# Index columns for the gathers of a graph kernel: one copy of all columns behind a step's first gather, in place of one copy behind each gather

## The chip, the cores and the metric

The kernel runs on one core of a Trainium2 chip, in one launch. The metric is the device time of the whole launch in microseconds. A run of the kernel before is 18072.75 us (median of three runs).

## The reference

The model works on a graph of 12,500 nodes and 412,500 edges that are sorted by their destination `dst`; the source `src` of an edge is a random node. Two graph networks run one after the other, each with a residual and a layer norm over the 16 features of a node. Cut to what matters here:

```python
# first network: two graph convolutions of 16 features
xw = x @ W.T
msg = xw[r] * norm[:, None]                      # r = src: a gather of one row per edge
out = jax.ops.segment_sum(msg, c, num_segments=num_nodes)

# second network: encoder, two rounds over the edges, decoder
for s in range(S):                               # S = 2
    ce = jnp.concatenate([e, n[senders], n[receivers]], axis=-1)
    e = e + _ln(_mlp(ce, ...), ...)              # n[senders]: again one row per edge
    agg = jax.ops.segment_sum(e, receivers, num_segments=num_nodes)
    cn = jnp.concatenate([n, agg], axis=-1)
    n = n + _ln(_mlp(cn, ...), ...)
```

Four passes over the edges fetch one table row for the source of every edge: two convolutions (rows of 16 floats) and two rounds (rows of 64 floats).

## The kernel before

The edges are cut into tiles of 128, one edge per partition, and eight tiles make a step (`G = 8`). A pass over the edges is one call of `edge_loop`, with 403 steps (`NIST`). There are four passes, and their tiles carry the names `g1` and `g2` (the convolutions) and `s0` and `s1` (the two rounds); the tiles of g1 and g2 both appear as `g_...` and those of s0 and s1 both as `s_...` in the profile, since numbers are left out of the names. Between the passes lie short phases over the nodes.

Each engine has its own program, a function `step(j, i, b)` that `drive` runs for every step: 19 steps are written out, then a loop on the device runs eight steps per turn, and the last steps are written out again. The engines work on different steps at one time (a lag such as `L_GA = 2` or `3` says how many steps later an engine handles a step), and meet only through semaphores. So in every pass each engine has a fixed order of work and waits for the others.

GpSimd (POOL in the profile) has one duty in a pass: to fetch the rows. For each tile it issues one indirect DMA (`L818`) which reads 128 rows of the table by the 128 node numbers in one column of an index tile `ix[k]`, and writes them to `gt[k]`. There are eight index tiles and eight row tiles, used in turn. The indices of all edges lie in `srcT` on chip; the column of a tile is at an address that depends on the step number. GpSimd therefore copies the columns to `ix`, whose addresses are fixed: behind the gather of tile `s` it copies column `s` of the next step (`L821`). The last copy of a step raises the semaphore `g_ix`.

Before its first gather a step waits (`done`, `landed`) for three things: that the rows in `gt[k]` from eight steps earlier have been used (`v_msg` in g1 and g2, `p_pre` in s0 and s1), that the indices of this step are there (`g_ix`), and that the gathers of seven steps ago have landed (`s_g`). `settle` is one semaphore instruction behind them.

In g1, s0 and s1 a step has eight gathers (`GA = 8`). In g2 it has five, since `xp = 3` tiles of a step take their rows by matmuls with a one-hot matrix from a table that is held on chip: VectorE (DVE) makes the one-hot `g_Oh` (L890), TensorE (PE) multiplies (L1008), DVE picks the rows (`g_sel`, L851, then L857).

Who uses the gathered rows: in g1 and g2 DVE multiplies them with the edge weights into `g_R` (L900); in s0 and s1 PE transposes them (L1033). PE's step in g1 begins with the matmuls of L1022, which need what DVE wrote for an earlier step (L920). Behind the last step of a pass GpSimd issues plain runs of gathers with no copies between them: L829 (`ahead`), and in the node phases L1154 and L1162 (`n_agg`); in the first phases of the kernel L521 (`NA`) is such a run too. `L823` is the copy that fills the first index tile of a pass in one operation.

Of the kernel before, what the change touches and what calls it, by code (L numbers as in the profile page):

```python
# [14 lines left out]
G = 8  # L15
# [45 lines left out]
def build(nc, a, out):  # L61
    ctx = ExitStack()
    with ctx:
        def sbuf(c, name, shape, dt=F32):
            return c.enter_context(nc.sbuf_tensor(name, shape, dt))
# [3 lines left out]
        def mark(name):  # L69
            return Mark(ctx.enter_context(nc.semaphore(name)))  # L70
# [36 lines left out]
        srcT = sbuf(ctx, "srcT", [128, NT + 8 * G], I32)  # L107
# [40 lines left out]
        def lasts_ahead(F):  # L148

            E = {80: 16, 64: 20, 16: 24}[F]  # L150
            return E, ahead[:, 0:E * F].rearrange("p (q f) -> p q f", f=F)
# [490 lines left out]
        def drive(eng, step, tail):  # L642

            for j in range(19):
                step(j, j // 8, j % 8)
            with eng.Fori(2, (NIST - 3) // 8) as i:
                for b in range(3, 11):
                    step(i * 8 + b, i, b)
            for j in range(NIST, NIST + tail):
                step(j, j // 8, j % 8)  # L650
# [5 lines left out]
        def stage(j, off):  # L656

            return not isinstance(j, int) or 0 <= j - off < NIST

        def done(eng, sem, j, off):  # L660

            v = j - (off - 1)
            if not isinstance(v, int) or v > 0:
                eng.wait_ge(sem.sem, v + sem.base)

        def landed(eng, sems, n, i, b, off):

            d = len(sems)
            gen = i * (8 // d) + (b - off) // d
            if not isinstance(gen, int) or gen >= 0:  # L670
                m = sems[(b - off) % d]
                eng.wait_ge(m.sem, (gen + 1) * (16 * n) + m.base)
# [7 lines left out]
        def settle(eng, sem):  # L680

            eng.sem_inc(sem, 1)
# [17 lines left out]
        g_ix, s_blank = mark("e_gix"), mark("e_blank")  # L700
# [3 lines left out]
        def edge_loop(tag, FG, table, seg_d, mlp=None, attr=False, expand=False, zsrc=None, zw=None, zout=None, ew2=None, counted=None, held=None, xp=0):  # L704


            L_GA = 2 if expand else 3
            L_LN, L_SEG = (6, 8) if mlp else (5, 6)
            L_ST = L_SUM = L_SEG + 1
            GA = G - xp  # L710
# [5 lines left out]
            with ExitStack() as c:  # L716
                def many(name, shape, dt=F32, n=2):
                    return [sbuf(c, f"{tag}_{name}{b}", shape, dt) for b in range(n)]
# [6 lines left out]
                ix = many("ix", [128, G], I32, n=8)  # L725
# [80 lines left out]
                def pool(eng):  # L806
                    def step(j, i, b):
                        if stage(j, L_GA):
                            k = (b - L_GA) % 8
                            if expand:  # L810
                                done(eng, p_pre, j, L_GA + 8)
                            else:
                                done(eng, v_msg, j, L_GA + 8)
                            done(eng, g_ix, j, L_GA)
                            landed(eng, s_g, GA, i, b, L_GA + 7)
                            settle(eng, s_m[1])
                            for s in range(GA):
                                eng.indirect_dma_start(out=gt[k][:, s, :], out_offset=None, in_=table[:, :],  # L818
                                                       in_offset=bass.IndirectOffsetOnAxis(ap=ix[k][:, s:s + 1], axis=0),
                                                       ).then_inc(s_g[k].sem, 16)  # L820
                                last = eng.tensor_copy(ix[(k + 1) % 8][:, s:s + 1], srcT[:, bass.ds((j - L_GA + 1) * G + s, 1)])  # L821
                            last.then_inc(g_ix.sem, 1)
                    eng.tensor_copy(ix[0][:, 0:GA], srcT[:, 0:GA]).then_inc(g_ix.sem, 1)  # L823
                    drive(eng, step, L_GA)
                    E, early = lasts_ahead(FS)
                    for k in range(2):
                        eng.wait_ge(*s_so[k](16 * (E * 128 // G // 2)))
                    for q in range(E):
                        eng.indirect_dma_start(  # L829
                            out=early[:, q, :], out_offset=None, in_=seg_d.rearrange("w t f -> (w t) f"),  # L830
                            in_offset=bass.IndirectOffsetOnAxis(ap=lidx[:, q:q + 1], axis=0)).then_inc(s_last[q // 4].sem, 16)
# [853 lines left out]
```

## Time and profile before

| | |
|---|---|
| runs of the kernel | 18072.75 us median of 3 (18071.34 to 18078.55) |
| the profiled execution's own time | 18121.37 us |
| its span, first to last instruction | 18119.2 us |
| GpSimd busy in it | 14425.3 us (80%) |
| TensorE busy | 13301.6 us (73%), mean granted clock 0.702 |
| VectorE busy | 9511.5 us (52%) |
| ScalarE busy | 3049.3 us (17%) |

Times in the profile are microseconds from the start of the span. A group of instructions is shown with its number, its busy time, the mean of one in nanoseconds, and then the time for which the engine stood idle just before them with what ended that idle time ("issue" is time in which the engine waited for nothing that the profile shows). Busy time counts the engine's own instructions; register, branch and semaphore instructions on the engine's sequencer (POOLq is that of GpSimd) are not in it. The chain that ended last is of little use in this kernel, since most of it lies in the last node phase; a pass is read from the waits inside it.

### The profile page before, as it was taken

What the parts mean: (1) busy time and instruction counts of PE and PEld (TensorE: products, weight loads), DVE (VectorE), ACT (ScalarE), POOL (GpSimd) and SP (SyncE); (2) the same over time, 40 slices, a digit from 0 to 9 for tenths busy, and PEclk for the clock granted to TensorE, in tenths of its full rate; (3) what the DMA queues carried; (4) which work ended last, traced back from release to release, by engine and by line L of the source; (5) the groups of instructions that cost most, each with busy time, mean ns of one, the idle gap of its engine ahead of it and who ended that gap; (6) DMA issues with size and microseconds to landing.
All of it is one profiled execution on the core that took longest, in us unless ns stands there. A gap on an engine that the chain in (4) does not pass through costs nothing. (4 is left out here: it accounts for less than half of the span.)

```text
span 18119.2 us, 353439 instructions
## 1 busy us (share of the span) xinstructions
PE 13301.6 (73%) x95144; PEld 10759.4 (59%) x95144; DVE 9511.5 (52%) x28331; ACT 3049.3 (17%) x5120; POOL 14425.3 (80%) x23987
## 2 busy tenths in 40 slices
PE   3777777777689999976777777767667667667775
PEld 2555555555479999974555555555545555555554
DVE  5444444444378888875445454445554444444444
ACT  1222222222200000001111111111111111111111
POOL 6888888888778888876888888888778888888886
PEclk5555555555589999996777777777776776777776
DMA  3222222222211111113555555555444444444442
GB/s 107 60 61 59 61 60 60 61 59 61 61 37 28 27 27 28 27 24 107 147 148 150 147 149 149 146 148 150 119 117 126 125 124 126 124 125 126 125 125 70
DMA packets 1973701, 1714.60 MB, mean 95 GB/s; under 512 B 1266475, under 2 KB 1436319, under 8 KB 1972431
## 3 DMA queue, kind: packets, MB, share of 16 engines
q10 hardware_dynamic: 939256, 958.97, 16.3%
q0 software_dynamic: 394560, 282.16, 9.7%
q1 hardware_dynamic: 639488, 469.70, 9.2%
q14 instruction: 333, 2.73, 0.0%
q8 instruction: 64, 1.05, 0.0%
HBM read 1096.56 MB, written 615.90 MB: 95 GB/s over the span
## 5 line engine op out<-in xcount | busy, mean ns | idle before, releaser
L818 POOL DMA_INDIRECT s_gt<-ta_d,s_ix x6448 | 6329.1, 982 | 1621.3 <-issue 967.9
L818 POOL DMA_INDIRECT g_gt<-xs_d,g_ix x3224 | 3158.7, 980 | 807.0 <-issue 483.6
L687 DVE TENSOR_TENSOR s_P<-psw,dlT 128x1024 f32<-128x1024 f32 x806 | 987.2, 1225 | 4106.8 <-PE psw L1055 4062.8
L1033 PE MATMUL pair<-ident,s_gt 128*128 128x128 f32 x3224 | 781.5, 389 | 2760.8 <-DMA s_gt<-ta_d,s_ix 2759.7
L1008 PE MATMUL pair<-g_part,g_Oh 128*128 128x224 bf16 x25389 | 2542.2, 261 | 238.9 <-DVE g_sel L851 211.7
L1008 PEld LDWEIGHTS pair<-g_part,g_Oh 128*128 128x128 bf16 x25389 | 2431.8, 99 | 279.4 <-issue 203.8
L1055 PEld LDWEIGHTS psw<-s_R,s_P 128*128 128x128 f32 x12896 | 2118.2, 247 | 734.3 <-issue 734.3
L818 POOL DMA_INDIRECT g_gt<-ys_d,g_ix x2015 | 1990.1, 988 | 583.6 <-POOL g_ix L821 325.6
L1033 PEld LDWEIGHTS pair<-ident,s_gt 128*128 128x128 f32 x3224 | 506.2, 194 | 3016.2 <-issue 1873.4
L1055 PE MATMUL psw<-s_R,s_P 128*128 128x64 f32 x12896 | 1998.8, 323 | 2.2 <-DVE s_R L920 1.4
L1055 PEld LDWEIGHTS psw<-g_R,g_P 128*128 128x128 f32 x6448 | 1405.3, 330 | 612.9 <-issue 612.9
L1022 PE MATMUL pair<-e_w,g_hT 128*128 128x128 f32 x3224 | 827.5, 438 | 1078.4 <-DVE g_R L920 1078.4
L900 DVE TENSOR_TENSOR g_R<-g_gt,ew 128x128 f32<-128x128 f32 x806 | 238.5, 296 | 2575.5 <-DMA g_gt<-xs_d,g_ix 2260.2
L1042 PE MATMUL pair<-s_z,zw 128*128 128x512 f32 x1612 | 1523.8, 1044 | 0.0
L1055 PE MATMUL psw<-g_R,g_P 128*128 128x80 f32 x6448 | 1491.8, 426 | 11.3 <-DVE g_R L920 11.3
L1022 PEld LDWEIGHTS pair<-e_w,g_hT 128*128 128x128 f32 x3224 | 717.6, 327 | 1234.6 <-issue 957.0
L821 POOL COPY s_ix<-srcT 128x1 int32 (+1 forms) x6448 | 1294.6, 201 | 41.1
L1039 PE MATMUL pair<-s_Pt,s_Bw 128*64 128x128 bf16 x19344 | 1124.2, 300 | 11.6 <-DVE s_Pt L882 11.6
L965 ACT ACTIVATE g_sg<-psw 128x640 f32<-128x640 f32 (+1 forms) x806 | 395.8, 491 | 4109.4 <-PE psw L1055 4090.3
L1039 PEld LDWEIGHTS pair<-s_Pt,s_Bw 128*64 128x64 bf16 x19344 | 938.1, 161 | 245.3 <-issue 194.1
L821 POOL COPY g_ix<-srcT 128x1 int32 (+1 forms) x5239 | 1052.7, 201 | 33.7
L960 ACT ACTIVATE s_hT<-pair 128x512 f32<-128x512 f32 x806 | 481.7, 598 | 3417.1 <-PE pair L1042 3404.8
(333 smaller groups left out, 18150.3 us busy)
## 6 DMA issues: line engine op xcount, KB each, us to landing
s_dl<-dl_d SPq DMA_DIRECT2D x404, 512.0 KB
seg_d<-s_sg ACTq DMA_DIRECT2D x806, 256.0 KB
s_Bw<-tb_d ACTq DMA_DIRECT2D x3224, 48.0 KB
s_Bw<-tb_d SPq DMA_DIRECT2D x3224, 48.0 KB
seg_d<-g_sg ACTq DMA_DIRECT2D x403, 320.0 KB
z_d<-g_rT ACTq DMA_DIRECT2D x403, 256.0 KB
s_z<-z_d ACTq DMA_DIRECT2D x403, 256.0 KB, 2.8
s_gt<-ta_d,s_ix POOLq DMA_INDIRECT x6448
```

The source lines that it names most:

```text
L687: return eng.tensor_tensor(P[:, :, :], bc(columns.rearrange("p (o e) -> p o e", o=1), [128, G, 128]), bc(dlT[:, bass.ds(j * G, G)].rearran ...
L818: eng.indirect_dma_start(out=gt[k][:, s, :], out_offset=None, in_=table[:, :], in_offset=bass.IndirectOffsetOnAxis(ap=ix[k][:, s:s + 1], a ...
L821: last = eng.tensor_copy(ix[(k + 1) % 8][:, s:s + 1], srcT[:, bass.ds((j - L_GA + 1) * G + s, 1)])
L900: last = eng.tensor_tensor(R[k][:, :, FM:FS], gt[k8][:, :, :], bc(ew2[:, bass.ds((j - L_LN) * G, G)].rearrange("p (s o) -> p s o", o=1), [ ...
L960: eng.activation(hT[k][:, :], ps[k][:, :], ACT.Silu).then_inc(a_h.sem, 1)
L965: eng.activation(sg[k][:, :].rearrange("p (t f) -> p t f", t=G), psw[:, 0:G * SP_].rearrange("p (t f) -> p t f", t=G)[:, :, 0:FS], ACT.Cop ...
L1008: last = eng.matmul(near_out(k, t), Oh[k][:, g, 128 * t:128 * t + 128], part[n][:, g, :, :].rearrange("p f l -> p (f l)"), start=g == 0 an ...
L1022: eng.matmul(ps[2 + k][:, 128 * q:128 * q + 128], hT[k][:, 128 * q:128 * q + 128], mlp[0][:, :], start=q == 0, stop=False, skip_group_chec ...
L1033: eng.matmul(ps[k][:, 128 * q:128 * q + 128], rows[:, 128 * q:128 * q + 128], ident[:, :], start=q == 0, stop=False, is_transpose=True, sk ...
L1039: eng.matmul(ps[k][64 * h:64 * h + 64, 128 * q:128 * q + 128], Bw[(b - L_PRE) % 4][:, t, 64 * n:64 * n + 64], Pt[k][:, 128 * t:128 * t + 1 ...
L1042: eng.matmul(ps[k][:, :], (e_w0 if attr else zw)[:, :], zt[(b - L_PRE) % DZ][:, :], start=not expand, stop=True, skip_group_check=True).th ...
L1055: last = eng.matmul(psw[:, SP_ * t:SP_ * t + FS], P[k][:, s, :], Rp[k][:, s, n, :] if thin else R[k][:, s, :], start=n == 0, stop=n == 2 o ...
```

## The change

GpSimd now copies all `GA` columns of the next step in one operation, directly behind the first gather of a step, and this copy raises `g_ix`. The other gathers of a step follow one another with nothing between them. The number of gathers, their data and all waits are as before.

```diff
--- before.py
+++ after.py
@@ -818,8 +818,8 @@
                                 eng.indirect_dma_start(out=gt[k][:, s, :], out_offset=None, in_=table[:, :],
                                                        in_offset=bass.IndirectOffsetOnAxis(ap=ix[k][:, s:s + 1], axis=0),
                                                        ).then_inc(s_g[k].sem, 16)
-                                last = eng.tensor_copy(ix[(k + 1) % 8][:, s:s + 1], srcT[:, bass.ds((j - L_GA + 1) * G + s, 1)])
-                            last.then_inc(g_ix.sem, 1)
+                                if s == 0:
+                                    eng.tensor_copy(ix[(k + 1) % 8][:, 0:GA], srcT[:, bass.ds((j - L_GA + 1) * G, GA)]).then_inc(g_ix.sem, 1)
```

The order of instructions on the other four engines is the same in both kernels. On GpSimd, this is the start of a step inside the device loop of g1 before the change. `DMA` is a gather; `ISA` and `REGISTER_ALU` are register instructions, which compute the column's address and the values to wait for; `e_vmsg`, `e_gix` and `e_g2` are the semaphores of the three waits named above.

```order
L664 REGISTER_ALU
L664 REGISTER_ALU [waits e_vmsg]
L818 DMA g_gt<-xs_d,g_ix 128x16 [waits e_gix,e_g2]
L821 ISA
L821 COPY g_ix<-srcT 128x1
L818 DMA g_gt<-xs_d,g_ix 128x16
L821 ISA
L821 COPY g_ix<-srcT 128x1
L818 DMA g_gt<-xs_d,g_ix 128x16
```

The gather and copy alternate to the step's end, so that the copy that raises `g_ix` stands right ahead of the next step's waits. The same step in the changed kernel, with the start of the next one:

```order
L664 REGISTER_ALU
L664 REGISTER_ALU [waits e_vmsg]
L818 DMA g_gt<-xs_d,g_ix 128x16 [waits e_gix,e_g2]
L822 ISA
L822 COPY g_ix<-srcT 128x8
L818 DMA g_gt<-xs_d,g_ix 128x16 x7
L664 REGISTER_ALU
L664 REGISTER_ALU [waits e_vmsg]
L818 DMA g_gt<-xs_d,g_ix 128x16 [waits e_gix,e_g3]
```

Seven copies and their seven address computations are gone, and seven gathers now stand between the copy and the wait for its semaphore. In g2 the loop of the changed kernel reads:

```order
L664 REGISTER_ALU
L664 REGISTER_ALU [waits e_vmsg]
L818 DMA g_gt<-ys_d,g_ix 128x16 [waits e_gix,e_g2]
L822 ISA
L822 COPY g_ix<-srcT 128x5
L818 DMA g_gt<-ys_d,g_ix 128x16 x4
```

There four copies and four address computations are gone from a step.

## Rows read from the trace of the kernel before

**Rows 1.** Instructions of line L818 in g1, g2, s0, s1: ns min/median/max, first and last start

```profile
L818 POOL DMA_INDIRECT g_gt<-xs_d,g_ix x3224: 974/979/6942, 246.7 to 4862.0; - x190
L818 POOL DMA_INDIRECT g_gt<-ys_d,g_ix x2015: 974/979/1204, 5064.0 to 8070.6; - x184
L818 POOL DMA_INDIRECT s_gt<-ta_d,s_ix x3224: 972/979/1242, 8327.7 to 12967.2; - x190
L818 POOL DMA_INDIRECT s_gt<-ta_d,s_ix x3224: 974/979/1574, 13209.8 to 17852.4; - x190
```

**Rows 2.** Waits in g1, g2 and s0: total us, times, longest

```profile
PE pair L1022 <- DVE g_R L920: 1078.4, 401, 10.6
DVE g_R L900 <- DMA g_gt<-ys_d,g_ix: 244.4, 202, 2.1
PE pair L1033 <- DMA s_gt<-ta_d,s_ix: 1359.2, 368, 18.5
POOL s_gt L818 <- PE pair L1042: 0.9, 6, 0.2
```

**Rows 3.** Timeline of GpSimd around one step in g1: start, duration, [idle before]

```profile
2059.06 0.97 POOL L818 DMA_INDIRECT g_gt<-xs_d,g_ix  x1 [0.81 <-POOL g_ix L821]
2060.05 0.19 POOL L821 COPY g_ix<-srcT 128x1 int32 x1
2061.23 0.98 POOL L818 DMA_INDIRECT g_gt<-xs_d,g_ix  x1 [1.00 <-issue]
...
2062.57 0.97 POOL L818 DMA_INDIRECT g_gt<-xs_d,g_ix  x1 [0.15 <-issue]
...
2069.23 0.98 POOL L818 DMA_INDIRECT g_gt<-xs_d,g_ix  x1 [0.15 <-issue]
2070.22 0.19 POOL L821 COPY g_ix<-srcT 128x1 int32 x1
2071.28 0.98 POOL L818 DMA_INDIRECT g_gt<-xs_d,g_ix  x1 [0.87 <-POOL g_ix L821]
```

**Rows 4.** Timeline of GpSimd, gathers in a row without copies (node phase)

```profile
13039.92 0.95 POOL L1162 DMA_INDIRECT n_agg<-seg_d,gidx  x1 [0.30 <-issue]
...
13044.93 0.95 POOL L1162 DMA_INDIRECT n_agg<-seg_d,gidx  x1 [0.31 <-issue]
```

**Rows 5.** Instructions of L823 in the whole span

```profile
L823 POOL COPY g_ix<-srcT x2: 191/192/192, 245.8 to 5063.0; 128x8 int32<-128x8 int32 x1, 128x5 int32<-128x5 int32 x1
```

**Rows 6.** Instructions of L821 from 2060.5 to 2070.3 us

```profile
L821 POOLq FUSED_REGOPS  x7: 46/46/46, 2061.0 to 2064.5; - x7
L821 POOL COPY g_ix<-srcT x7: 192/193/201, 2062.2 to 2070.2; 128x1 int32 x7
```

**Rows 7.** Busy us of the engines in g1, g2, s0, then clock, DMA share, GB/s

```profile
246.70:4863.30 4616.60, 3533.47 (x12472) 2646.48 (x12473) 1965.80 (x6433) 1329.22 (x2011) 3789.68 (x6448) 0.50 0.22 60
5063.90:8071.60 3007.70, 2767.43 (x35037) 2726.89 (x35037) 2526.04 (x6879) 111.65 (x402) 2411.62 (x4030) 0.98 0.16 29
8327.60:12968.30 4640.70, 3279.04 (x23629) 2586.82 (x23629) 2306.68 (x6888) 716.15 (x1201) 3809.75 (x6448) 0.74 0.53 148
```

**Rows 8.** Timeline of TensorE in g2

```profile
6042.43 6.20 PE L1008 MATMUL pair<-g_part,g_Oh 128*128 128x224 bf16 x63
...
6049.07 6.20 PE L1008 MATMUL pair<-g_part,g_Oh 128*128 128x224 bf16 x63
```

**Rows 9.** Groups by line: L521 in the span, L1022 in g1, L1022 in s0

```profile
L521 POOL DMA_INDIRECT NA<-tab_d,tidx x98 | 102.5, 1046 | 30.1 <-issue 30.1
L1022 PE MATMUL pair<-e_w,g_hT 128*128 128x128 f32 x3224 | 827.5, 438 | 1078.4 <-DVE g_R L920 1078.4
L1022 PE MATMUL pair<-e_w,s_hT 128*128 128x128 f32 x3208 | 501.1, 308 | 0.0
```

**Rows 10.** Timeline of GpSimd, first gathers of the run at L521

```profile
74.72 1.11 POOL L521 DMA_INDIRECT NA<-tab_d,tidx  x1 [0.51 <-issue]
...
96.90 1.43 POOL L521 DMA_INDIRECT NA<-tab_d,tidx  x1 [0.31 <-issue]
98.63 1.45 POOL L521 DMA_INDIRECT NA<-tab_d,tidx  x1 [0.30 <-issue]
```

## Prediction before the run

> **What bounds the kernel now.** I read first how long each pass takes and how evenly GpSimd's gathers run through it, then who waits for whom inside a pass, then single steps. From the first to the last gather g1 takes 4862.0 - 246.7 = 4615.3 us, s0 4639.5, s1 4642.6 and g2 3006.6 [rows 1]. Together these are 16,904 of the span's 18,119 us, so almost all the time is passes. A pass has 403 steps. In the three with eight gathers, first to last gather is 3223 spacings, or 402.9 steps: 11.456 us per step in g1, 11.516 in s0, 11.524 in s1. In g2 it is 2014 spacings, 402.8 steps, 7.464 us each.
>
> The waits say who sets this pace. In s0 PE stands idle for gathered rows for 1359.2 us, 3.37 us a step, and in g1 PE waits 1078.4 us, 2.68 a step, for what DVE makes out of gathered rows; GpSimd waited for PE 0.9 us in the whole of s0 [rows 2]. So in g1, s0 and s1 nobody holds GpSimd up, and everybody waits for it. PE is busy 3533.47 / 403 = 8.77 us a step in g1 and 3279.04 / 403 = 8.14 in s0; DVE 1965.80 / 403 = 4.9 and 5.7 [rows 7]. Each lies far below 11.5.
>
> Now one step of GpSimd [rows 3]. A gather takes 0.98, its copy 0.19, and then 0.15 us pass before the next gather: six spacings from 2061.23 to 2069.23 are 8.00 us, 1.334 each. Behind the last copy the gap is not 0.15 but 0.81 to 0.87 (2.01 us from gather to gather, taking 0.84 for the gap), and the row names the copy as what ended it: the copy's semaphore `g_ix` must arrive before the waits of the next step are passed, and only then is the gather prepared. Once per turn of the device loop, every eight steps, one more spacing is long: 2061.23 - 2059.06 = 2.17, so 0.84 over 1.334, with "issue" named. Sum: 7 x 1.334 + 2.01 + 0.84 / 8 = 11.45, against 11.456 measured in g1. So the step is accounted for, and all of it is GpSimd's.
>
> Two things on the sequencer matter for what follows. The address computations for seven copies were all done between 2061.0 and 2064.5, while the copies themselves ran until 2070.2 [rows 6]: the sequencer prepares a gather and a copy in (2064.5 - 2061.0) / 6 = 0.58 us and runs far ahead of the engine until it meets the `g_ix` wait, where it stands until 2070.4. So inside a step the spacing is the engine's and not the sequencer's, and at each boundary the lead is lost.
>
> **The change, part by part.** (a) The first gather and its copy stay. The copy is wider, but a copy of 128x8 or 128x5 took 0.192 us [rows 5] and of 128x1 0.193 [rows 6]: no cost. The spacing behind the first gather stays 1.334.
>
> (b) Between the other gathers the copy goes. Its busy time is 0.19, but that is not what is won. Gathers with nothing between them are in the trace: from 13039.92 to 13044.93 there are four spacings, 1.252 each, 0.95 of gather and 0.30 of gap [rows 4]. The gap grows from 0.15 to 0.30 when the copy is gone, so a removed copy gives 1.334 - 1.252 = 0.082 us. These are 64-float rows as in s0 and s1; no row is needed for 16 floats, since L818 has a median of 979 ns for both [rows 1]. Six spacings: 0.49 us a step.
>
> The Trainium skill, Trace Analysis, "GPSIMD Engine Instruction", says that a GpSimd span in a profile is unreliable and that start-to-start spacing is to be used. Here the trace agrees: adding up durations would credit 0.19 for each copy, some 0.11 us too much on each of 6 x 1209 spacings, about 800 us, and the forecast would be about 15,470 us in place of the one below.
>
> (c) The boundary. The last copy goes, and the copy that raises `g_ix` was executed seven gathers earlier, some 8.8 us. The other waits are long satisfied (0.9 us of waiting in s0). The sequencer is held at the `g_ix` wait of the next step only until the copy behind the present first gather is done; from there it leads by seven gathers. It needs at most 0.58 us per gather against 1.252 of the engine, so it keeps the lead, and the register instructions (46 ns) and waits of the boundary hide behind running gathers. So this spacing becomes 1.252 too: 2.01 - 1.252 = 0.76 us a step.
>
> (d) The long spacing once per turn (0.84 us) appears where the sequencer has just lost its lead. With a lead of several gathers it is covered: 0.105 us a step. What hides it is the queued gathers; if they are not queued that deep, 0.105 x 1209 = 127 us come back.
>
> New step in g1: 1.334 + 7 x 1.252 = 10.10 us. The first gather of g1 is 6.94 long [rows 1], 6 us that stay. s0 and s1 are now 0.060 and 0.068 above g1 per step, which I put down to brief blocking beside busier engines, and keep: 10.16 and 10.17. Times 402.9: g1 4075, s0 4093, s1 4097; saved 540, 546 and 545, together 1631 us.
>
> (e) What is late next. In g1 PE needs 8.77 us of 10.10, in s0 8.14 of 10.16: their waits shrink from 2.68 to about 1.3 and from 3.37 to about 2.0, and GpSimd still sets the pace. In g2 it is different. GpSimd could do 1.334 + 4 x 1.252 = 6.34 us a step. But DVE waits there only 244.4 us for rows in 202 waits [rows 2], and some 0.34 us of each such gap is there in the steps without a wait as well: (244.4 - 202 x 0.34) / 403 = 0.44 us a step is all that faster gathers can give. DVE, coupled with PE over `g_sel`, then sets the step at 7.464 - 0.44 = 7.03: 176 us saved. The bound below is PE when nothing holds it: 6049.07 - 6042.43 = 6.64 us [rows 8], 157 us more.
>
> **Sum.** 1631 + 176 = 1807 us. The profiled execution took 18121 (span 18119) and its span is what I summed; the median of the runs is 48 lower. The node phases do not change, so I take the difference off the median: 18,072.75 - 1807 = 16,266 us. Its own range: down to 16,060 if g2 falls to PE's 6.64 and the 0.06 us in s0 and s1 vanish with the copies (157 + 48 us); up to 16,440 if the spacing per turn stays and that blocking doubles (127 + 48).
>
> **Rivals.**
> B: the boundary is not hidden. The nearest row is a gather that the sequencer prepares with no queued one ahead of it and no wait: gap 0.51 [rows 10]. The step is then 1.334 + 6 x 1.252 + (0.95 + 0.51) + 0.105 = 10.41, about 1257 us saved in the three passes, with g2 1433: 16,640 us. If the whole 0.81 gap stays, 363 us more: 17,003. For it: there are three waits and up to four register instructions there; against it: [rows 6].
>
> C: inside a pass gathers in a row are slower than in a quiet phase, since DVE works beside them. The run at L521 has mean 1046 ns with 0.307 of gap, a spacing of 1.353 [rows 9]: step 10.81, saving 832 + 176: 17,065 us. Against it: with all engines busy L818 is at 979 median and 1.2 to 1.6 us at most after the first gather [rows 1]. The Trainium skill, SBUF, "A bandwidth-pool intuition that's wrong (but worth ruling out)", says that GpSimd cannot write descriptors while DVE holds the port pair they share, and gives about 620 ns against 3100; no gather of s0 or s1 is that long, so the trace shows at most short blocking.
>
> D: another engine becomes the bound in s0 and s1. PE's granted clock is 0.50 in g1 and 0.74 in s0 [rows 7], and the same 128x128 f32 matmul takes 438 ns and 308 [rows 9]. If s0 and s1 fell to g1's clock, PE's 8.14 would be 8.14 x 438 / 308 = 11.6 us a step and nothing would be gained there: 540 + 176 saved, 17,357 us. Against it: PE gets denser work, and in g2, where it is busy 92% of the time, the clock is 0.98.
>
> E, the other side: a gather directly behind another has to wait for its descriptors or packets under the load of the passes (DMA share 0.53 in s0 [rows 7]), and the copies were a useful distance. The worst pair in the trace is 96.90 to 98.63, 1.73 us, 1.75 with the next row's 1.45 + 0.30 [rows 10]; with 1.74 a step is 13.51 and g2's 8.29, 2770 us more: 20,843 us. It decides from a spacing of (11.5 - 1.334) / 7 = 1.45 us upward. Nothing in the passes points there.
>
> **How the numbers follow.** Forecast 0.76, B 0.10, C 0.05, D 0.04, E 0.02, and 0.03 for still faster than 16,030 (gathers closer than 1.252). The range 16,030 to 16,700 holds the forecast's own range with some margin and the nearer two thirds of B, about 0.8. A measurement of this kernel tells about 0.2% from no change. Only E lies above; faster 0.97, within 0.2% 0.01, slower 0.02.
>
> **What the changed kernel's profile would show.** GpSimd: 1612 copies at L822 of about 0.19 us; gathers of 0.95 with gaps of 0.30, also at the first gather of a step, with no `g_ix` named; no 1.00 us gap per turn. First to last gather of g1 near 4070 us, s0 and s1 near 4095, g2 near 2830. PE's wait at L1033 in s0 about 2.0 us a step and at L1022 in g1 1.3. In g2 DVE's wait for rows nearly gone, and GpSimd waiting there for `v_msg`, that is for DVE. I am wrong at (c) if gaps over 0.5 stay at the boundaries, at (b) if gathers space at 1.3 or more, at (e) if g2's step is far from 7.03 or GpSimd waits in s0.

## The result, and the profile after

| | before | changed |
|---|---|---|
| median of the runs | 18072.04 us (18070.26 to 18078.55) | 16182.78 us (16180.15 to 16213.33, 4 runs) |
| ratio | 1 | 0.8958, 95% interval 0.8942 to 0.8973 |
| the profiled execution | 18121.37 us | 16213.33 us |

The changed kernel is 10.4% faster: 1889 us between the medians. The forecast was 16,266 us, 1807 us saved, so it came out 83 us above the measured time. The page of the changed kernel gives the span, and what each engine was busy in it:

```profile
span 16211.2 us, 333764 instructions
PE 12601.8 (78%) x95144; PEld 10226.0 (63%) x95144; DVE 9452.5 (58%) x28331; ACT 3026.7 (19%) x5120; POOL 12104.2 (75%) x13912
```

GpSimd's busy time fell from 14425 to 12104 us, 2321 us, and the span by 1908. Neither figure follows from the other. A removed copy is 0.19 us of busy time and gives 0.08 us of spacing, and the pauses that went at the boundaries of steps were not busy time at all.

The four passes, in the instructions of the gather's line (columns as in [rows 1]; windows of the changed kernel around g1, g2, s0 and s1):

```profile
L818 POOL DMA_INDIRECT g_gt<-xs_d,g_ix x3224: 941/947/6943, 246.3 to 4337.0; - x190
L818 POOL DMA_INDIRECT g_gt<-ys_d,g_ix x2015: 942/947/1202, 4538.4 to 7273.1; - x184
L818 POOL DMA_INDIRECT s_gt<-ta_d,s_ix x3224: 941/947/1593, 7541.2 to 11628.9; - x190
L818 POOL DMA_INDIRECT s_gt<-ta_d,s_ix x3224: 941/947/1477, 11868.6 to 15944.8; - x190
```

Last start minus first start, against the same of [rows 1]:

| pass | before | forecast | after | per step | saved: forecast, measured |
|---|---|---|---|---|---|
| g1 | 4615.3 | 4075 | 4090.7 | 10.15 | 540, 524.6 |
| g2 | 3006.6 | 2830 | 2734.7 | 6.79 | 176, 271.9 |
| s0 | 4639.5 | 4093 | 4087.7 | 10.15 | 546, 551.8 |
| s1 | 4642.6 | 4097 | 4076.2 | 10.12 | 545, 566.4 |

The last column adds up to 1807 forecast and 1914.7 measured in the profiled executions. Of the difference of 108 us, 96 are g2's. The time outside the passes grew by 7 us (1914.7 - 1908.0 of span). The profiled executions lie 49 and 31 us above their medians, which takes off the remaining 19 us down to 1889.

One step of GpSimd in g1 now, from the timeline of the changed kernel, answers to [rows 3]:

```profile
2007.42 0.95 POOL L818 DMA_INDIRECT g_gt<-xs_d,g_ix  x1 [0.30 <-issue]
2008.38 0.20 POOL L822 COPY g_ix<-srcT 128x8 int32 x1
2008.74 0.98 POOL L818 DMA_INDIRECT g_gt<-xs_d,g_ix  x1 [0.16 <-POOL g_ix L822]
2010.02 0.95 POOL L818 DMA_INDIRECT g_gt<-xs_d,g_ix  x1 [0.30 <-issue]
...
2017.53 0.95 POOL L818 DMA_INDIRECT g_gt<-xs_d,g_ix  x1 [0.30 <-issue]
```

The first gather of a step is the one ahead of the copy, at 2007.42. The gap in front of it is 0.30 us, as in front of any other; before the change it was 0.81 to 0.87. From 2007.42 to 2017.53 are eight spacings: 1.32 over the copy, 1.28 for the next, and six of 1.25, together 10.11 us. The 1.28 is the one thing that the forecast's spacings did not have: the gather behind a copy itself takes 0.98 in place of 0.95, with a full gap of 0.30 behind it. In turn the spacing over the copy is 1.32 and not 1.334, since the gather ahead of the copy takes only 0.95.

The copies themselves, and what the sequencer did about the copy at 2008.38 (instructions of L822 in the span, and of L682, the `settle`, from 2008 to 2018.7 us; ns min/median/max, first and last start):

```profile
L822 POOL COPY g_ix<-srcT x806: 195/201/387, 253.3 to 7268.9; 128x5 int32 x77, 128x8 int32 x76, 128x8 int32<-128x8 int32 x5, 128x5 int32<-128x5 int32 x4
L822 POOL COPY s_ix<-srcT x806: 195/201/506, 7542.1 to 15936.9; 128x8 int32 x154, 128x8 int32<-128x8 int32 x8
...
L682 POOLq EVENT_SEMAPHORE  x1: 43/43/43, 2008.6 to 2008.6; - x1
```

There are 1612 copies of a median 201 ns. The sequencer passes the waits of the next step at 2008.6, as soon as the copy of this step has ended and one gather into the step, and then has seven gathers' time in hand.

Busy time by engine in g1, g2, s0 and s1 (columns as in [rows 7]):

```profile
246.30:4338.30 4092.00, 3532.74 (x12467) 2645.78 (x12468) 1956.10 (x6433) 1329.02 (x2010) 3165.25 (x3628) 1.00 0.25 67
4538.30:7274.10 2735.80, 2693.15 (x34522) 2667.51 (x34523) 2441.04 (x6780) 109.72 (x395) 2028.46 (x2418) 1.00 0.18 31
7541.10:11629.90 4088.80, 2959.86 (x23618) 2327.70 (x23619) 2300.02 (x6881) 698.68 (x1199) 3161.67 (x3627) 0.80 0.59 168
11868.50:15945.80 4077.30, 2913.60 (x22021) 2233.49 (x22022) 2050.54 (x6484) 709.96 (x1199) 3150.21 (x3627) 0.76 0.52 142
```

And the waits of the changed kernel, the first row from the window of g1, the next two from that of s0, the others from g2's (total us, times, longest):

```profile
PE pair L1022 <- DVE g_R L920: 555.6, 401, 10.2
...
PE pair L1033 <- DMA s_gt<-ta_d,s_ix: 1053.5, 264, 18.1
POOL s_gt L818 <- PE pair L1042: 3.7, 12, 0.3
...
POOL g_gt L818 <- issue: 698.0, 1969, 0.8
DVE g_R L900 <- issue: 126.9, 380, 0.5
PE pair L1008 <- DVE g_sel L851: 3.0, 12, 0.4
```

In g1 and s0 PE still waits for rows or for what is made of them (1.38 and 2.61 us a step), and GpSimd for hardly anybody (3.7 us in the whole of s0): it is still the bound. In g2 the wait of DVE for gathered rows, 244.4 us in [rows 2], is gone. PE is busy 2693 of 2736 us there and DVE waits only a short, unnamed 0.33 us a step, so these rows alone leave open which of the two bounds g2.

### The profile page after: what moved, and what is told of

It is laid out like the page before. It is cut to its first block and busy times, and to the rows that moved or that the text cites. A ratio compares the mean times of both kernels' runs of the same rounds, so it can differ in the third digit from the quotient of the medians.

```text
span 16211.2 us, 333764 instructions
## 1 busy us (share of the span) xinstructions
PE 12601.8 (78%) x95144; PEld 10226.0 (63%) x95144; DVE 9452.5 (58%) x28331; ACT 3026.7 (19%) x5120; POOL 12104.2 (75%) x13912
## 3 DMA queue, kind: packets, MB, share of 16 engines
q8 instruction: 64, 1.05, 0.0%
## 5 line engine op out<-in xcount | busy, mean ns | idle before, releaser
L818 POOL DMA_INDIRECT s_gt<-ta_d,s_ix x6448 | 6149.5, 954 | 1852.4 <-issue 1713.4
L818 POOL DMA_INDIRECT g_gt<-xs_d,g_ix x3224 | 3084.2, 957 | 925.8 <-issue 861.7
L1008 PE MATMUL pair<-g_part,g_Oh 128*128 128x224 bf16 x25389 | 2500.0, 259 | 47.7 <-DVE g_Oh L890 22.2
L818 POOL DMA_INDIRECT g_gt<-ys_d,g_ix x2015 | 1947.3, 966 | 706.3 <-issue 698.0
L1008 PEld LDWEIGHTS pair<-g_part,g_Oh 128*128 128x128 bf16 x25389 | 2406.8, 98 | 73.8 <-issue 51.0
L1033 PE MATMUL pair<-ident,s_gt 128*128 128x128 f32 x3224 | 707.6, 359 | 2201.1 <-DMA s_gt<-ta_d,s_ix 2200.3
L1055 PEld LDWEIGHTS psw<-s_R,s_P 128*128 128x128 f32 x12896 | 1927.6, 228 | 634.4 <-issue 634.4
L1055 PE MATMUL psw<-s_R,s_P 128*128 128x64 f32 x12896 | 1828.7, 304 | 2.0 <-DVE s_R L920 1.2
L1042 PE MATMUL pair<-s_z,zw 128*128 128x512 f32 x1612 | 1343.2, 928 | 0.0
L900 DVE TENSOR_TENSOR g_R<-g_gt,ew 128x128 f32<-128x128 f32 x806 | 241.4, 299 | 1876.3 <-DMA g_gt<-xs_d,g_ix 1745.3
L1022 PE MATMUL pair<-e_w,g_hT 128*128 128x128 f32 x3224 | 827.6, 438 | 555.6 <-DVE g_R L920 555.6
L1022 PEld LDWEIGHTS pair<-e_w,g_hT 128*128 128x128 f32 x3224 | 717.8, 328 | 711.7 <-issue 545.0
L951 ACT ACTIVATE s_sq<-pair 128x512 f32<-128x512 f32 x806 | 481.5, 597 | 3127.5 <-issue 2561.8
L1022 PE MATMUL pair<-e_w,s_hT 128*128 128x128 f32 x6448 | 974.2, 299 | 17.7 <-DVE s_R L920 17.0
L1039 PE MATMUL pair<-s_Pt,s_Bw 128*64 128x128 bf16 x19344 | 972.5, 272 | 13.0 <-DVE s_Pt L882 13.0
L687 DVE TENSOR_TENSOR g_P<-pair,dlT 128x1024 f32<-128x1024 f32 (+1 forms) x806 | 980.5, 1216 | 0.0
```

The costliest lines, as they stand in the source:

```text
L687: return eng.tensor_tensor(P[:, :, :], bc(columns.rearrange("p (o e) -> p o e", o=1), [128, G, 128]), bc(dlT[:, bass.ds(j * G, G)].rearran ...
L900: last = eng.tensor_tensor(R[k][:, :, FM:FS], gt[k8][:, :, :], bc(ew2[:, bass.ds((j - L_LN) * G, G)].rearrange("p (s o) -> p s o", o=1), [ ...
L951: eng.activation(sq[k][:, :, :].rearrange("p s f -> p (s f)"), ps[2 + k][:, :], ACT.Square).then_inc(a_sq.sem, 1)
L1008: last = eng.matmul(near_out(k, t), Oh[k][:, g, 128 * t:128 * t + 128], part[n][:, g, :, :].rearrange("p f l -> p (f l)"), start=g == 0 an ...
L1022: eng.matmul(ps[2 + k][:, 128 * q:128 * q + 128], hT[k][:, 128 * q:128 * q + 128], mlp[0][:, :], start=q == 0, stop=False, skip_group_chec ...
L1033: eng.matmul(ps[k][:, 128 * q:128 * q + 128], rows[:, 128 * q:128 * q + 128], ident[:, :], start=q == 0, stop=False, is_transpose=True, sk ...
```

## The experiments

**Theory.** A copy costs its effect on the spacing (0.08 us), and the wait at the boundary costs 0.8 us only as long as the copy that raises `g_ix` is the last thing ahead of it; a lead of the sequencer hides it, and the pause once per turn of the loop with it. In g2 DVE sets the step. **Rivals.** The number of copies is what counts, wherever they stand. Or the boundary costs nothing by itself, and the wide copy is what helps. In g2: PE sets the step, or GpSimd still does.

The before kernel has a median of 18,117 us on the chip of the first four experiments, 18,075 on the next four runs' and 18,101 on the last one's. Times are therefore compared by ratio, or within one chip. Each diff is against the changed kernel. Steps, spacings and rows are those of the profiled execution.

### The copy behind the last gather

```diff
-                                if s == 0:
+                                if s == GA - 1:
```

> One copy of all columns per step, as in the changed kernel, but behind the last gather of the step in place of the first. Theory (a removed copy gives back only 0.082 us of spacing; the rest of the gain is that the g_ix semaphore is raised long before the next step waits for it): inside a step gathers space at 1.252 us, the boundary keeps a gap of 0.81 to 0.87 us, and the long spacing once per turn of the loop (0.84 us in eight steps) stays: 7 x 1.252 + 2.01 + 0.105 = 10.88 us a step against 10.12 now in g1, s0 and s1, and 7.12 against 6.79 in g2. Total about 17,220 us. Rival (the copies' own time of 0.2 us each, 2,014 us in all, is what was won): almost nothing comes back, 16,200 to 16,300 us.

Measured: 17226.71 us (17222.75 to 17228.5), ratio 0.9508 (0.9492 to 0.9523). The timeline of GpSimd in g1 of this kernel:

```profile
2008.39 0.21 POOL L822 COPY g_ix<-srcT 128x8 int32 x1
2009.41 0.97 POOL L818 DMA_INDIRECT g_gt<-xs_d,g_ix  x1 [0.81 <-POOL g_ix L822]
...
2020.15 0.97 POOL L818 DMA_INDIRECT g_gt<-xs_d,g_ix  x1 [0.81 <-POOL g_ix L822]
...
2054.43 0.94 POOL L818 DMA_INDIRECT g_gt<-xs_d,g_ix  x1 [1.08 <-issue]
```

The gap of 0.81 us at the boundary is back, with as few copies as in the changed kernel. The steps are 10.87 us in g1, 10.88 in s0, 10.90 in s1 and 7.11 in g2. So the number of copies is not the whole matter: their place is worth 0.055 of the ratio, about 1,000 us, and fewer copies alone 0.049. The long spacing once per turn is back too: one step in eight begins with a spacing of 2.05 us in the mean against a usual 1.28, with the gap of 1.08 at 2054.43 as one case. So steps (c) and (d) go by the same lead.

### Single columns, the last one early

The columns are copied one by one again, two behind the first gather and none behind the last, so that the semaphore is raised one gather ahead of the boundary.

```diff
-                                if s == 0:
-                                    eng.tensor_copy(ix[(k + 1) % 8][:, 0:GA], srcT[:, bass.ds((j - L_GA + 1) * G, GA)]).then_inc(g_ix.sem, 1)
+                                for c in {0: (0, 1)}.get(s, (s + 1,) if s < GA - 1 else ()):
+                                    last = eng.tensor_copy(ix[(k + 1) % 8][:, c:c + 1], srcT[:, bass.ds((j - L_GA + 1) * G + c, 1)])
+                                if s == GA - 2:
+                                    last.then_inc(g_ix.sem, 1)
```

> Single-column copies as in the kernel before, as many, but each one gather earlier: two behind the first gather, none behind the last, so that the copy that raises g_ix has one gather behind it. Theory (the wait at the boundary is most of the gain and one gather is enough to hide it): a step of eight gathers is 1.53 + 6 x 1.334 + 1.252 = 10.79 us, or 10.89 if the long spacing per turn stays, against 11.46 to 11.52 in the kernel before; g2 6.8 to 6.9. Total 17,000 to 17,160 us. Rival (copy durations are the gain, the boundary gives nothing): about 18,070 us, as the kernel before.

Measured: 17024.8 us (16961.31 to 17041.79), ratio 0.9400 (0.9384 to 0.9416). The four runs spread more than those of the other kernels, and the profiled one is the lowest. Its timeline of GpSimd over a boundary in g1; the first gather of a step is the one at 2008.19:

```profile
2006.91 0.98 POOL L818 DMA_INDIRECT g_gt<-xs_d,g_ix  x1 [0.15 <-POOL g_ix L822]
2008.19 0.95 POOL L818 DMA_INDIRECT g_gt<-xs_d,g_ix  x1 [0.30 <-issue]
2009.14 0.31 POOL L822 COPY g_ix<-srcT 128x1 int32 x2
2009.60 0.97 POOL L818 DMA_INDIRECT g_gt<-xs_d,g_ix  x1 [0.15 <-issue]
```

All the copies are there as before the change, and 6.0% is gained by moving them: the boundary costs a gap of 0.30. The steps are 10.73 us in g1 and 10.80 in s0 and s1. The second copy in a row costs 0.08 us once more (1.41 from 2008.19 to 2009.60, against 1.33 over one copy). Of the pause per turn a part stays: once in eight steps the 1.41 is 1.76 in g1 and 1.68 in s0 and s1, in the mean. The rival by which the boundary is free falls. Of the whole 10.4%, somewhat more than half is the boundary's, whichever part is taken out first (6.0% with all copies kept, 5.5% with few), and the rest that of the copies.

### The copy behind the second last gather

```diff
-                                if s == 0:
+                                if s == GA - 2:
```

> One copy of all columns per step, behind the second last gather. It tells how much lead is needed: with the copy behind the first gather seven gathers lie between copy and wait, here one. Theory: one gather (1.25 us) covers the 0.8 us that the boundary costs, but not the longer pause of the sequencer once per turn, which needs more lead: 0 to 0.1 us a step slower than the changed kernel, 16,180 to 16,310 us. Rival (lead of several gathers is needed at each boundary): gaps of 0.5 us stay there, 0.2 us a step more in 1209 steps, 16,430 us or more.

Measured: 16230.11 us (16220.01 to 16231.53), ratio 0.8958 (0.8943 to 0.8973), the changed kernel's own ratio. Timeline of GpSimd in g1 of this kernel:

```profile
2012.84 0.20 POOL L822 COPY g_ix<-srcT 128x8 int32 x1
2013.20 0.98 POOL L818 DMA_INDIRECT g_gt<-xs_d,g_ix  x1 [0.16 <-POOL g_ix L822]
2014.48 0.94 POOL L818 DMA_INDIRECT g_gt<-xs_d,g_ix  x1 [0.30 <-issue]
2015.90 0.94 POOL L818 DMA_INDIRECT g_gt<-xs_d,g_ix  x1 [0.47 <-issue]
```

One gather between the copy and the boundary covers the wait as well as seven do. The place behind the first gather is not what matters, only that it isn't behind the last. Where the lead is so short, a remainder of the pause per turn shows: 0.47 at 2015.90 in place of 0.30, 0.17 us once in eight steps. It is smaller than in the kernel with single columns, which has one gather of lead too; why is open. The step of g2 is 6.82 us here.

### The old copies in g2 alone

```diff
-                                if s == 0:
+                                if xp:
+                                    last = eng.tensor_copy(ix[(k + 1) % 8][:, s:s + 1], srcT[:, bass.ds((j - L_GA + 1) * G + s, 1)])
+                                    if s == GA - 1:
+                                        last.then_inc(g_ix.sem, 1)
+                                elif s == 0:
```

> The changed kernel with the code of before in g2 alone (single columns, g_ix raised by the last of them). The change in g1, s0 and s1 stays. Theory: g2 goes back from 2735 to 3007 us and nothing else moves: 16,183 + 272 = 16,455 us. Rival (g2's gain came from elsewhere, such as how full the chip's other engines were): g2 well below 3000 us.

Measured: 16475.59 us (16470.75 to 16478.08), ratio 0.9094 (0.9079 to 0.9109). The gather's line in g2 of this kernel:

```profile
L818 POOL DMA_INDIRECT g_gt<-ys_d,g_ix x2015: 974/979/1197, 4537.5 to 7542.7; - x184
```

That is 3005.2 us, as before the change (3006.6), while g1, s0 and s1 keep 10.15, 10.14 and 10.12 us a step. So g2's pace does not act on the other passes, and g2's share of the gain is 0.0136 of 18,117, or 246 us, by the ratios; 260 us by the profiles of this kernel and the one with the copy behind the second last gather, whose g2 has 2745.3.

### The changed kernel on another chip

> The changed kernel once more, unaltered, as the reference for the other kernels of this call on the same chip, since the kernel before differs by some 45 us from chip to chip. 16,180 to 16,230 us.

Measured: 16178.27 us (16176.8 to 16178.97), ratio 0.8950 (0.8935 to 0.8965). That is 2 us below the range expected. The steps are 10.12 us in g1, 10.11 in s0, 10.10 in s1 and 6.78 in g2. The 10.15 of g1 in the first profile is 0.03 above this; the kernel with the old copies in g2 has 10.15 too, so from execution to execution g1 differs by that much.

### One copy for four steps

The eight index tiles become one tensor, and a copy of 128x32 behind the first gather of every fourth step fills four of them. The wait for landed gathers is then made in that step for four steps at once. The diff is cut to what matters.

```diff
-                            done(eng, g_ix, j, L_GA)
-                            landed(eng, s_g, GA, i, b, L_GA + 7)
+                            eng.wait_ge(g_ix.sem, i * 2 + (b - L_GA) // 4 + 1 + g_ix.base)
+                            if k % 4 == 2:
+                                for n in range(3, 7):
+                                    landed(eng, s_g, GA, i, b, L_GA + n)
...
-                                if s == 0:
-                                    eng.tensor_copy(ix[(k + 1) % 8][:, 0:GA], srcT[:, bass.ds((j - L_GA + 1) * G, GA)]).then_inc(g_ix.sem, 1)
+                                if s == 0 and k % 4 == 2:
+                                    at = (k + 2) % 8 * G
+                                    eng.tensor_copy(ixs[:, at:at + 4 * G], srcT[:, bass.ds((j - L_GA + 2) * G, 4 * G)]).then_inc(g_ix.sem, 1)
```

> All columns of four steps in one copy (32 columns), behind the first gather of every fourth step, two gathers' worth of steps ahead of their use; g_ix is raised once per copy and the wait for landed gathers of three to six steps ago stands only in the steps that copy. Theory (a copy between two gathers costs 0.06 us of spacing and the gather behind it 0.03 to 0.05 more, whatever its width; GpSimd still sets the pace in g1, s0 and s1): three of four copies go, 0.75 x 0.11 us x 1209 steps, 80 to 110 us faster than the changed kernel; g2 unchanged at 6.79 us a step. Rival (another engine sets the pace already): no difference.

Measured: 16084.5 us (16081.55 to 16105.98), ratio 0.8897 (0.8882 to 0.8912): 94 us below the changed kernel's 16178.27 on the same chip, and the fastest version that does all the work. Copy and neighbours, from the timeline of GpSimd in g1:

```profile
2042.28 0.22 POOL L826 COPY g_ix<-srcT 128x32 int32 x1
2042.66 1.05 POOL L821 DMA_INDIRECT g_gt<-xs_d,g_ix  x1 [0.16 <-issue]
2044.01 0.94 POOL L821 DMA_INDIRECT g_gt<-xs_d,g_ix  x1 [0.30 <-issue]
```

The step is 10.064 us in g1 against 10.120, so 0.056 is won there; s0 and s1 win 0.054 and 0.057. In the changed kernel a copy costs 0.07 in the spacing over it and 0.03 in the next one, 0.10 a step. Here it costs 2042.66 - 2041.33 - 1.25 = 0.08 and 2044.01 - 2042.66 - 1.25 = 0.10, together 0.18 in four steps; 0.10 - 0.18 / 4 = 0.055. The three passes win 67 us together, and g2 gives 7 more, which is near the 72 us between the two profiled executions (16178.11 and 16105.98); the medians lie 94 apart, since the latter lies 21 above its median. The expectation had the cost of a copy independent of its width. It is not: the gather behind 32 columns takes 1.05 us and behind eight 0.98, and so a copy costs 0.18 us against 0.10.

### g2 with less work on PE

Of the three bf16 parts of the held table only two are multiplied; the third part of the rows is left out.

```diff
-                                for n in range(3):
+                                for n in range(2):
...
-                                                      start=g == 0 and n == 0 and t % 2 == 0, stop=g == GN - 1 and n == 2,
+                                                      start=g == 0 and n == 0 and t % 2 == 0, stop=g == GN - 1 and n == 1,
```

> The changed kernel, but in g2 TensorE multiplies only two of the three bf16 parts of the table (42 matmuls in place of 63 a step); the low bits of the rows that come this way are left out. It asks who sets g2's 6.79 us a step. Theory (VectorE: in the changed kernel it works without a wait): no difference, within 10 us. Rival (TensorE, which is busy 98% of g2): TensorE's step falls by 2 us and g2 to GpSimd's 6.4 us, 150 us faster.

Measured: 16178.16 us (16174.91 to 16197.74), ratio 0.8949 (0.8934 to 0.8964), equal to the changed kernel's on this chip. From the waits of this kernel in g2, 4600 to 7200 us:

```profile
PE pair L1008 <- DVE g_sel L851: 596.3, 378, 2.3
```

PE has a third less of L1008's matmuls and waits for DVE in their place: 596.3 us where the changed kernel has 3.0 in its whole g2. PE is busy 2089 us of g2 in place of 2693, and the step is 6.785 us against 6.782. PE does not bound g2, though it was busy for 98% of it.

### g2 with more work on DVE

The first cast of g2's rows is done twice.

```diff
+                        eng.tensor_copy(Rp[k][:, :, 0, :], R[k][:, :, :])
+                        eng.drain()
                         eng.tensor_tensor(rest[:, :, :], R[k][:, :, :], Rp[k][:, :, 0, :], ALU.subtract)
```

> The changed kernel with one VectorE instruction more per step in g2: the first cast of the message (L862, 0.23 us and 0.07 us of drain) is done twice. Theory (VectorE sets g2's pace): 403 x 0.30 = 121 us slower than the changed kernel. Rival (TensorE or the gathers set it): under 40 us slower.

Measured: 16318.18 us (16310.47 to 16321.76), ratio 0.9028 (0.9013 to 0.9043), 140 us above the changed kernel. The step of g2 grows by 0.33 us, to 7.11: the cast's 0.23 us, 0.07 of gap beside it, and 0.03 more, which is what the second cast (L866, here L868) takes longer: 266 ns in place of 231. From its waits in g2, 4600 to 7200 us:

```profile
POOL g_gt L818 <- DVE g_Rp L870: 370.1, 339, 1.4
```

The whole of the added DVE work lengthens g2's step, and GpSimd waits for DVE to free the row tiles. Together with the run before it: DVE bounds g2.

### Seven gathers in place of eight

In g1, s0 and s1 the gather of one of eight tiles is left out, and its rows are zeros. The kernel computes something else; it only tells how far away the next bound is. The waits for landed gathers count seven in place of eight, which the diff leaves out.

```diff
-                            for s in range(GA):
+                            for s in [n for n in range(GA) if xp or n != 3]:
```

> The changed kernel with one gather left out of each step of g1, s0 and s1 (tile 3; its rows are zeros, so the edges of that tile get wrong data), to see how far away the next bound is. Theory (GpSimd still sets the pace, TensorE needs 8.8 us a step in g1 and 7.3 in s0 and s1): a step falls by one spacing of 1.25 us to 8.87, 1209 x 1.25 = 1,511 us faster than the changed kernel, about 14,670 us. Rival (TensorE or VectorE sets the pace by now in some pass): less than 1,300 us faster.

Measured: 14683.52 us (14682.97 to 14684.3), ratio 0.8112 (0.8098 to 0.8125) against 18,101 on this chip. The gather's line in g1:

```profile
L819 POOL DMA_INDIRECT g_gt<-xs_d,g_ix x2821: 940/945/6603, 246.3 to 3820.3; - x189
```

That is 3574.0 us for 402.9 steps, 8.87 us each, where the sum by spacings gives 10.12 - 1.25 = 8.87; s0 has 8.89 and s1 8.86. So in the changed kernel the gathers alone set the pace in these passes: each is still worth its full 1.25 us, and no second bound was met down to 8.87 us a step. The expectation had counted on 8.8 us of PE in g1, which would have left 0.1. The window of g1 shows less (columns as in [rows 7]):

```profile
246.30:3821.30 3575.00, 3098.02 (x12456) 2369.03 (x12456) 1975.75 (x6433) 1309.32 (x2010) 2771.07 (x3224) 0.61 0.26 76
```

PE is busy 3098.02 / 403 = 7.69 us a step for the same matmuls. The granted clock is 0.61 here and L1022's matmul (L1025 in this kernel) takes 419 ns in the mean in place of 438, so a part of g1 ran at the upper clock in this kernel.

## Why the prediction was right, and where it was off

**(a) The wide copy.** Right: 0.20 us for eight columns against 0.19 for one, and the spacing over it 1.31 to 1.33 us. What it did not say is that the gather behind a copy is 0.03 longer (1.28 in place of 1.25), some 12 us a pass; the shorter spacing over the copy gives about half of it back.

**(b) The removed copies, 0.082 us each.** Right, by the six spacings of 1.25 and by the copies taken out alone (one copy for four steps). The rule that it was weighed with, of the Trainium skill, Perfetto Trace Analysis, "GPSIMD Engine Instruction" (go by the distance of starts, not by the spans), agrees with this: by durations it would have been 15,470 us, 700 too few.

**(c) The boundary, 0.76 us a step.** Right, and shown from both sides: the gap comes back with the copy moved behind the last gather, and goes with all copies kept when the last of them is one gather earlier. The lead of seven gathers that the working speaks of is more than is needed: one hides the boundary.

**(d) The pause per turn.** Right: covered by a lead of seven gathers, nearly whole (0.77 us) without a lead, and with a lead of one gather 0.17 to 0.35 us of it stay.

**The three passes.** The 1631 us forecast for g1, s0 and s1 became 1642.8, but not pass by pass: g1 gave 15 us less than forecast and s1 21 more, since the 0.06 us a step that the forecast had kept as blocking in s0 and s1 does not show in s1 any more. So the close sum is in part luck.

**(e) g2.** The bound was named rightly, DVE, and the size was off. The forecast was a step of 7.03 us and 176 us saved; measured are 6.79 and 272, and these 96 us are nearly all of the error. The term that was too small is "0.44 us a step is all that faster gathers can give". DVE's wait for rows did fall by that: 312.7 / 402 - 129.6 / 396 = 0.45 us a step. But the forecast put two other things at nothing. The first is the length of DVE's own instructions. These are one-hots, L900 and the second cast in g2, of the kernel before, of the changed kernel, and of the one with single columns early (count, busy, mean ns, idle before):

```profile
L890 DVE TENSOR_SCALAR g_Oh<-g_dl,iog 128x384 bf16<-128x384 f16 x2821 | 757.9, 338 | 11.4 <-PE pair L1008 7.3 <-DMA g_dl<-hp_d 4.1
L900 DVE TENSOR_TENSOR g_R<-g_gt,ew 128x128 f32<-128x128 f32 x402 | 120.2, 299 | 312.7 <-DMA g_gt<-ys_d,g_ix 244.4 <-issue 56.5 <-PE psw L1055 9.9
L866 DVE CAST g_Rp<-g_rest 128x128 bf16<-128x128 f32 x402 | 105.3, 262 | 29.7 <-issue 0.3
```

```profile
L890 DVE TENSOR_SCALAR g_Oh<-g_dl,iog 128x384 bf16<-128x384 f16 x2786 | 719.9, 327 | 11.4 <-PE pair L1008 6.3 <-DMA g_dl<-hp_d 5.1
L900 DVE TENSOR_TENSOR g_R<-g_gt,ew 128x128 f32<-128x128 f32 x396 | 116.1, 293 | 129.6 <-issue 126.9 <-PE psw L1055 1.0
L866 DVE CAST g_Rp<-g_rest 128x128 bf16<-128x128 f32 x396 | 91.8, 232 | 29.0
```

```profile
L892 DVE TENSOR_SCALAR g_Oh<-g_dl,iog 128x384 bf16<-128x384 f16 x2814 | 702.3, 317 | 11.3 <-PE pair L1010 6.9 <-DMA g_dl<-hp_d 4.4
```

Seven one-hots shorter by 11 ns, L866 by 30, L900 by 6 and the first cast (L862) by 10 are 0.12 us a step. The second thing is how far GpSimd runs ahead of DVE. DVE's own step is read from all 403 starts of L900 in g2, before and after:

```profile
L900 DVE TENSOR_TENSOR g_R<-g_gt,ew x403: 291/293/366, 5093.2 to 8073.1; 128x128 f32<-128x128 f32 x135
L900 DVE TENSOR_TENSOR g_R<-g_gt,ew x403: 291/293/361, 4567.3 to 7316.0; 128x128 f32<-128x128 f32 x135
```

These are 7.41 and 6.84 us a step, 0.57 less, which is the 0.45 and the 0.12. GpSimd's step fell by 0.67, because it now ends the pass seven steps ahead of DVE and before only one (396 and 402 of the 403 L900 lie in the windows); six steps of 6.84 are 41 us. So the 272 us are 181 of waiting, 50 of shorter instructions and 41 of lead. The lead is not all gain: behind g2 GpSimd stands 18.07 us in front of L1154 and before 5.78, and the first gather of s0 follows the last one of g2 after 268.1 us in place of 257.1. These 11 us are what the time outside the passes grew by, less some 4 us gained elsewhere.

The traces show when a DVE instruction is slow. It is not the number of GpSimd's copies that counts: the last row of one-hots above has as many copies as before and is the shortest. It is where the instruction falls against a gather. An L866 of the kernel before that starts 0.54 us behind a gather:

```profile
5476.59 0.98 POOL L818 DMA_INDIRECT g_gt<-ys_d,g_ix  x1 [0.16 <-issue]
5477.13 0.47 DVE L866 CAST g_Rp<-g_rest 128x128 bf16<-128x128 f32 x1
```

Of its 402 L866, 98 start 0.50 to 0.80 us behind the start of a gather. These take 369 ns in the mean; the other 304 take 227, and none of them more than 236. In the changed kernel only 15 of 396 start there, which is the whole difference of L866. Of the one-hots 533 start there before (422 ns, the others 318) and 428 after (411, the others 312), so they follow it in part. This is read from the starts in the traces and no experiment was made on it; what in a gather does it, no run here shows. DVE's step without late rows is therefore no constant: by the starts of L900 it is 6.84 us in the changed kernel, 6.81 with one copy for four steps, 6.76 with single columns early and 6.86 with the copy behind the second last gather, with 0.33 of idle time before L900 in each.

**The other marks.** PE's wait in g1 was forecast at 1.3 us a step and is 1.38. In s0 it was forecast at 2.0 and is 2.61, since PE's busy time fell from 8.14 to 2959.86 / 403 = 7.34 us a step; it changed nothing, since GpSimd is the bound. GpSimd waiting in g2 shows in the changed kernel only as unnamed time (0.8 at most, 698 us in all): the spacing at the boundary is 1.69 us in the mean in place of 1.25. That it is for DVE was made visible by the run with more DVE work.

**The rivals.** B (boundary not hidden) did not happen; a kernel with the boundary left open does exist and took 17,227 us on its chip. C (gathers slowed beside a busy DVE) did not: the median gather of the passes takes 947 ns and the spacing is 1.25. What the traces show is the other way round, some of DVE's instructions slow beside gathers, and only in g2 is DVE the bound. D (PE the bound in s0 and s1) did not: PE was busy 7.34 us a step of s0, and even with seven gathers the pace stayed GpSimd's. E (copies as a useful distance) did not: no spacing of 1.45 us or more in the steps shown, and s0 and s1 with their 0.52 to 0.59 DMA share run like g1.

## What to carry to other kernels

Where one engine feeds the others with instructions of about a microsecond, look at its spacings from start to start and find those that are longer than the rest; here one in eight held more than half of the gain. A semaphore that an engine raises for its own next wait belongs at least one long instruction ahead of that wait, and that alone was worth 6%, with all the work kept. Old step minus wait is not a safe floor for the engine that comes next: here its own instructions became 0.12 us a step shorter as well, and an engine that runs ahead finishes its part of a pass early, so each engine's step is to be read from its own starts. A run with less and one with more work on one engine tell which of two busy engines is the bound, where 98% busy does not.

## What had not been expected of the hardware

The granted clock that the views give for g1 is 0.50 before the change [rows 7] and 1.00 after it, which would be 1.2 GHz in one and 2.4 GHz in the other. The matmuls do not follow. L1022 in g1 of the changed kernel:

```profile
L1022 PE MATMUL pair<-e_w,g_hT 128*128 128x128 f32 x3224 | 827.6, 438 | 555.6 <-DVE g_R L920 555.6
```

It has the same mean of 438 ns as in [rows 9], and PE's busy time in g1 is 3532.7 us against 3533.5. The kernel with the copy behind the last gather shows 1.00 and the one with single columns early 0.50, and both have 438 ns again. The reason is a missing record. In the trace of the kernel before, one record of 0.50 lasts from 20.2 to 5085.6 us. The trace of the changed kernel has no clock record at all before 4371.1 us, and that of the copy behind the last gather none before 4656.4; a stretch without a record is counted as 1.00. The Trainium skill, TensorE: Matmul & The Clock Gate, "Seeing it yourself", calls the trace's clock events unreliable at times and advises a check against another measure; this trace agrees, by the two rows with 438 ns.

The other measure is L1022 itself. In s0 of the kernel before, both levels are on record; these are a window of each (for L1022 alone: us, busy us of PE and PEld, clock, DMA share, GB/s) and its matmuls in them:

```profile
12083.00:12100.00 17.00, 1.92 (x8) 1.83 (x8) 0.50 0.39 109
L1022 PE MATMUL pair<-e_w,s_hT x8: 421/421/421, 12092.4 to 12093.9; 128*128 128x128 f32 x8
12021.60:12035.10 13.50, 2.11 (x16) 1.94 (x16) 1.00 0.62 174
L1022 PE MATMUL pair<-e_w,s_hT x16: 275/275/275, 12022.7 to 12031.8; 128*128 128x128 f32 x16
```

In g1 no L1022 of either kernel is shorter than 421 ns, so PE ran g1 at the lower level, 1.2 GHz, in both. Rival D was priced by 438 and 308 ns, which are the matmuls' own times, and that price stands; the mean granted clock of a whole kernel with such a missing stretch is too high. In s0, where the records are there, they and the matmuls agree: the clock rose from 0.74 to 0.80, PE's busy time fell from 8.14 to 7.34 us a step, and L1022 went from 308 to 292 ns.

The price of GpSimd's small copies was also smaller than any duration suggests. 0.20 us of work between two gathers moves them only 0.05 to 0.08 us further apart, since the gap before the gather shrinks from 0.30 to 0.15 or 0.16 at the same time. The gather behind the copy is longer on top of that: 0.98 us behind one or eight columns and 1.05 behind 32, in place of 0.95. Together a copy costs 0.08 us with one column, 0.10 with eight and 0.18 with 32.
